# The first group's query and key rows copied inside SBUF, head by head, and four projections moved into the first run of score maxima

## The reference

```
q, k, v = x @ wq.T + bq, x @ wk.T + bk, x @ wv.T + bv     # 16 heads of 8
scores  = einsum('bhqd,bhkd->bhqk', q, k) * 1/sqrt(16)
out     = einsum('bhqk,bhkd->bhqd', softmax(scores), v)
x = layernorm(x + out @ wo.T + bo)
h = silu(x @ w1.T * s1) * (x @ w2.T * s2)                 # 512 wide
h = gelu(h @ h1.T * sh1); h = gelu(h @ h2.T * sh2)
x = layernorm(x + h @ w3.T * s3)
```

## Time and profile before

| What | Value |
|---|---|
| median of 3 runs | 471.40 us (471.39 to 471.72) |
| the profiled execution | 472.66 us, of which the span of the trace is 470.9 us |
| mean granted TensorE clock | 0.992 of full speed |
| PE, DVE, ACT, POOL busy | 450.0, 394.0, 365.5, 86.7 us |
| DMA traffic | 24.48 MB |

### The profile page before, as it was taken

The page is one execution under the profiler, slowest core; times in us unless marked ns, Lnnn a source line. Parts: engine busy times, 40 slices in busy tenths (PEclk is TensorE's granted clock), DMA queues, the critical chain, the costliest instruction groups (busy, mean ns, idle before and its releaser), DMA issues.

```text
span 470.9 us, 9453 instructions
## 1 busy us (share of the span) xinstructions
PE 450.0 (96%) x3630; PEld 213.1 (45%) x3632; DVE 394.0 (84%) x442; ACT 365.5 (78%) x678; POOL 86.7 (18%) x138
## 2 busy tenths in 40 slices
PE   8899999999999999999999999999899799998992
PEld 5333343333333333333343333434343478776882
DVE  6899999999999999999999999999753347647435
ACT  3402898989889899898988989999868786588671
POOL 8400000000000010000000001362511262037002
PEclk9999999999999999999999999999999999999998
...
DMA packets 15547, 24.48 MB, mean 52 GB/s; under 512 B 4560, under 2 KB 8400, under 8 KB 15120
## 3 DMA queue, kind: packets, MB, share of 16 engines
...
...
## 4 chain that ended last, share of the span: by engine, by line
PE 77%; DVE 11%; ACT 5%; issue 2%; POOL 2%; DMA 2%; ACTq 0%; POOLq 0%; DVEq 0%
PE ps L1036 31%; PE ps L1090 29%; PE ps L1174 11%; DVE negmax L798 8%; PE ps L1073 2%; ACT arena L542 2%; DMA qx<-parts_q 1%; ACT hid L582 1%; DVE hf L889 1%; ACT v_pad L576 1%; PE ps L992 1%; PE ps L1123 1%; DVE stats L844 1%; PE ps L1001 1%; ACT hid L592 1%
## 5 line engine op out<-in xcount | busy, mean ns | idle before, releaser
L798 DVE TENSOR_REDUCE negmax<-ps 128x1 f32<-128x1024 f32 x256 | 309.5, 1223 | 6.6 <-PE ps L1036 3.6
L542 ACT ACTIVATE arena<-ps 128x512 f32<-128x512 f32 x512 | 275.1, 597 | 38.9 <-PE ps L1073 15.8
L1036 PE MATMUL ps<-kx,qx 61*128 61x512 f32 x512 | 186.3, 443 | 2.3 <-DMA qx<-parts_q 1.3
L1073 PE MATMUL ps<-qx,kx 64*128 64x512 f32 x512 | 182.2, 450 | 0.0
L1090 PE MATMUL ps<-arena,v_pad 128*32 128x256 f32 x2048 | 163.8, 392 | 1.1 <-ACT arena L542 1.1
L1036 PEld LDWEIGHTS ps<-kx,qx 61*128 61x128 f32 x512 | 75.4, 184 | 101.3 <-DVE negmax L798 85.6
L1090 PEld LDWEIGHTS ps<-arena,v_pad 128*32 128x32 f32 x2048 | 40.5, 108 | 88.1 <-issue 51.3
L1073 PEld LDWEIGHTS ps<-qx,kx 64*128 64x128 f32 x512 | 75.7, 184 | 8.2 <-issue 4.9
L1174 PE MATMUL ps<-hid,w_high 128*128 128x512 f32 (+1 forms) x296 | 67.6, 386 | 1.1 <-ACT hid L592 1.0
L1174 PEld LDWEIGHTS ps<-hid,w_high 128*128 128x128 f32 x296 | 54.3, 188 | 12.6 <-ACT hid L592 1.8
L898 DVE TENSOR_TENSOR hid<-hf,hid 128x512 fp32r<-128x512 f32 x32 | 21.9, 689 | 25.4 <-ACT hid L592 25.4
...
## 6 DMA issues: line engine op xcount, KB each, us to landing
...
```

The lines of the kernel that those rows point to most:

```text
L542: nc.scalar.activation(probs[:, n // HG % 2, heads(n), :], ps[:, PLAN["score", n][0], :], ACT.Exp, scale=SCALE).then_inc(exp_done, 1)
L798: nc.vector.tensor_reduce(negmax[:, t // TURNS % 2, h * QT + q:h * QT + q + 1], ps[:, bank:bank + 2, :], AX.XY, ALU.max, negate=True)\
L1036: ins = nc.tensor.matmul(ps[:, MAX_BANK + 2 * (t % 2) + part, :], qx[at, slot, qc, h, q * P:(q + 1) * P], kx[at, slot, h, part * C:(part + ...
L1073: nc.tensor.matmul(ps[:, bank, :], kx[at, slot, h % PAIR, kt * P:(kt + 1) * P], qx[at, slot, qc, h % PAIR, :], start=True, stop=True)\
```

## The change

Line numbers in this section are those of the changed program where they stand behind a +.

- The first group's rows are no longer stored to DRAM and loaded back. `spread_k` and `spread_q` copy them from SBUF to SBUF, one transfer for each head and part: 8 rows at the source, each read twice, 16 rows at the destination. SP issues 8 for k (64 KB each) and 8 for q of chunk 1 (32 KB each); ACT issues 8 for q of chunk 0 (32 KB each), of which four stand ahead of its fourth high part.
- The first 16 turns take the heads one after the other (`FIRST_HEADS` = 0, 2, 1, 3), and each head has a semaphore (`head_in`), which counts its four transfers.
- Projections 5 to 8 move from ahead of the first turn to behind turns 1, 4, 7 and 10 (`LATE_JOBS`), where they stand in for the fillers; the turn after one has no fillers.
- PE's six fillers wait for the fourth low part. DVE adds the bias of v ahead of that fourth split.
- The two memsets of slot 1 of `qx` go from DVE to POOL, behind `stage_v`.
- The low and high parts lie together in one tensor, `parts`; SP's stores for the other groups are six (k, and q of both chunks) where four stood at this place.

The diff (left out: the move of buffers and semaphore names, and the definition of `store_q_first`, which goes):

```diff
@@ -145,10 +145,14 @@
+FIRST_HEADS = (0, 2, 1, 3)
 WARM, FILL = 9, 6
+LATE_JOBS = (1, 4, 7, 10)
 
 
 def head_of(t):
+    if t < TURNS:
+        return FIRST_HEADS[t // QT], t % QT
@@ -181,18 +187,16 @@
-               for n, at in enumerate((ARENA, ARENA + SLOT_BYTES, ARENA + 2 * SLOT_BYTES, ARENA + 5 * SLOT_BYTES))]
+               for n, at in enumerate((ARENA, ARENA + SLOT_BYTES, ARENA + 2 * SLOT_BYTES, ARENA + 6 * SLOT_BYTES))]
 
         qx = nc.alloc_sbuf_tensor_at("qx", [P, 2, QC, PAIR, C], F32R, offset=ARENA)
         kx = nc.alloc_sbuf_tensor_at("kx", [P, 2, PAIR, L], F32R, offset=ARENA + 2 * QC * PAIR * C * 4)
-        low = arena[0][:, 8 * PAIR * L:].bitcast(F32).rearrange("p (n t) -> p n t", n=2)
 
         attn = arena[1][:, 0:2 * U_ALL * C].bitcast(F32).rearrange("p (u c) -> p u c", c=C)
         probs = arena[1][:, 2 * U_ALL * C:].bitcast(F32).rearrange("p (s h c) -> p s h c", s=2, h=HG)
 
-        prt = sb("prt", [P, 4 * TOK], BF16)
-        high = prt[:, 0:4 * TOK].bitcast(F32).rearrange("p (n t) -> p n t", n=2)
-        part = {n: (high[:, a], low[:, a]) for a, n in enumerate("qk")}
+        parts = nc.alloc_sbuf_tensor_at("parts", [P, HALVES, 2, TOK], F32, offset=ARENA + 2 * SLOT_BYTES)
+        part = {n: (parts[:, 1, a], parts[:, 0, a]) for a, n in enumerate("qk")}
@@ -308,6 +313,12 @@
+        def spread_q(eng, h, j, qc, done):
+
+            at = h // PAIR * GROUP + j * HALVES * DH
+            eng.dma_start(qx[at:at + HALVES * DH, 0, qc, h % PAIR, :].bitcast(F32),
+                          parts[h * DH:(h + 1) * DH, :, 0, qc * C:(qc + 1) * C]).then_inc(done, 16)
+
@@ -370,24 +381,29 @@
-            sp.wait_ge(split_high, 2)
-            store_k(0, 0, 0, 1, k_first)
+            def spread_k(h, j):
+
+                at = h // PAIR * GROUP + j * HALVES * DH
+                sp.dma_start(kx[at:at + HALVES * DH, 0, h % PAIR, :].bitcast(F32),
+                             parts[h * DH:(h + 1) * DH, j, 1, 0:L].unsqueeze(1).broadcast_to([DH, HALVES, L]))\
+                  .then_inc(head_in[h], 16)
+
             sp.wait_ge(split_low, 2)
-            store_k(0, 1, 0, 1, k_first)
-            sp.wait_ge(k_first, STORE_INC)
-            load_k(0, 0)
+            for h in FIRST_HEADS:
+                for j in range(HALVES):
+                    spread_k(h, j)
             sp.wait_ge(split_low, 4)
-            sp.wait_ge(rows_in[0][0], LOAD_INC[0])
-            for i in range(HALVES):
-                store_q(1, i, 0, NG, q_out[1])
-            sp.wait_ge(q_out[1], STORE_INC)
-            load_q(0, 0, 1)
+            for h in range(HG):
+                for j in range(HALVES):
+                    spread_q(sp, h, j, 1, rows_in[0][1])
             for j in range(HALVES):
                 store_k(0, j, 1, NG, k_out[0])
-            for i in range(HALVES):
-                store_q(0, i, 1, NG, q_out[0])
+            for c in range(QC):
+                for i in range(HALVES):
+                    store_q(c, i, 1, NG, q_out[c])
             sp.wait_ge(k_out[0], STORE_INC)
-            sp.wait_ge(q_out[0], STORE_INC)
+            for c in range(QC):
+                sp.wait_ge(q_out[c], STORE_INC)
@@ -517,17 +527,13 @@
-                    act.wait_ge(split_high, n + 1)
-                    store_q_first(0)
-            act.wait_ge(split_low, 3)
-            store_q_first(1)
-            act.wait_ge(q_first, STORE_INC)
-            for r in range(2):
-                for i in range(HALVES):
-                    at = r * GROUP + i * HALVES * DH
-                    act.dma_start(qx[at:at + HALVES * DH, 0, 0].bitcast(F32),
-                                  q_dram[i, 0, 0, r * PAIR:(r + 1) * PAIR].rearrange("h d j t -> (d j) h t"))\
-                       .then_inc(rows_in[0][0], 16)
+                    act.wait_ge(split_low, n + 1)
+                    for h in FIRST_HEADS[:PAIR]:
+                        for j in range(HALVES):
+                            spread_q(act, h, j, 0, head_in[h])
+            for h in FIRST_HEADS[PAIR:]:
+                for j in range(HALVES):
+                    spread_q(act, h, j, 0, head_in[h])
@@ -684,6 +690,12 @@
+            for r in range(2):
+                at = slice(r * GROUP + ROWS, (r + 1) * GROUP)
+                if r == 0:
+                    pool.wait_ge(v_staged, 2)
+                nc.gpsimd.memset(qx[at, 1].bitcast(F32), 0.0).then_inc(rows_set_late, 1)
+                pool.wait_ge(rows_set_late, r + 1)
@@ -773,7 +785,7 @@
-            for n in range(EARLY):
+            for n in range(EARLY - 1):
@@ -785,7 +797,7 @@
-            no_rows(1)
+            split(EARLY - 1)
@@ -1017,10 +1029,8 @@
-            for n in range(EARLY, len(JOBS)):
-                job(n)
-            pe.wait_ge(proj_ready, 1)
-            busy(FILL, FIRST_BANKS[1])
+            pe.wait_ge(split_low, EARLY)
+            busy(FILL, JOB_BANKS[-1])
@@ -1030,9 +1040,14 @@
-                    if t % TURNS == 0:
-
-                        pe.wait_ge(rows_in[slot][qc], (t // (PER * TURNS) + 1) * LOAD_INC[qc])
+                    if t < TURNS and t % QT == 0:
+                        pe.wait_ge(head_in[FIRST_HEADS[t // QT]], 64)
+                    elif t % (PER * TURNS) == 0:
+                        pe.wait_ge(rows_in[slot][qc], t // (PER * TURNS) * LOAD_INC[qc])
+                    elif t % TURNS == 0:
+
+                        first = LOAD_INC[1] if (slot, qc) == (0, 1) else 0
+                        pe.wait_ge(rows_in[slot][qc], (t // (PER * TURNS) + 1) * LOAD_INC[qc] + first)
@@ -1100,14 +1115,20 @@
-                busy(1, FIRST_BANKS[1])
-                busy(1, FIRST_BANKS[1], C // 2)
+                if t in LATE_JOBS:
+                    job(EARLY + LATE_JOBS.index(t))
+                elif t - 1 not in LATE_JOBS:
+                    if t > LATE_JOBS[-1]:
+                        pe.wait_ge(proj_ready, 1)
+                    bank = JOB_BANKS[0 if t > LATE_JOBS[-1] else -1]
+                    busy(1, bank)
+                    busy(1, bank, C // 2)
                 if t == TURNS + 2:
 
                     pe.wait_ge(ident_ready, 3)
                     pe.wait_ge(proj_ready, EARLY)
                     turn_max(0)
-            pe.wait_ge(rows_set, 4)
+            pe.wait_ge(rows_set_late, 2)
```

13 lines of the change are left out of this document (6 added, 7 removed).

## The result

The changed kernel is slower: 474.69 us median (473.46 to 492.66, 5 runs) against 471.39 (471.01 to 471.72, 5 runs), a ratio of 1.006 [1.0044, 1.0076]. This ratio leaves out the executions near 492 us, as a disturbed run would be left out, though here they belong to the kernel (the experiments show it): over all executions of the changed kernel on record they were 7 of 16. Predicted was 468.9, with a range of 468.3 to 472.4.

The account below looks back on a forecast made before the run. A lead-in of the first turn's time plus 23 turns at DVE's pace, then a PE-bound loop. Gain 3.2 less 0.7 for moved projections is 2.5 us, taking the median from 471.4 to 468.9; range 468.3 to 472.4.

Parts of the forecast that it names:

- the first term: Lead-in: four ACT issues at 0.67 us each let the first turn start at 15.4 instead of 18.61, gaining 3.2 us.
- no earlier turn: Rival, lead-in: slow issues or a late fourth transfer keep the first turn from coming earlier; 470.5 to 471.5, chance 0.08.
- The rival of the clock: Lead-in: PE's 1.5 us pause drops the clock, leaving 0.5 to 0.9 us of gain; 469.8 to 471, chance 0.2.
- What follows here is dense: Argument against a clock fall in the lead-in: fillers and full-width products follow PE's 1.5 us pause.
- What the moved projections cost: Behind turns 1, 4, 7 and 10: DVE waits 0.4 us once, then 0.1 each; 0.7 us, bounds 0.2 and 1.3.
- The moved memsets: Lead-in: moving two memsets from DVE to POOL costs nothing; POOL spends 2 x 1.8 us between 12.4 and 16.1.
- SP's queue: Ahead of the loop: stores end between 31.0 and 33.2, ahead of 33.7; costed at nothing, bounds 0 and 5 us.
- the copies didn't hold the stores: Denies the rival that copies ending at 31.2 delay stores and loop start; 471.4 to 476, chance 0.12.
- Head 0's q: Lead-in: head 0's rows complete at 13.8, needed at 15.4, so the first turn doesn't wait for them.
- the first half of the prediction: Lead-in up to the first turn: fillers start at 14.1 and the first turn at 15.4 instead of 18.61.

Follow-up runs that it names:

- e10: Changed kernel with SP's eight transfers of k held back until ACT has issued its first four transfers of q; 494.26 us in one run.
- the trace of 473.38: A later execution of the changed kernel, with no edit, traced; 473.38 us.
- e2: Changed kernel with ACT's fourth high part ahead of all its transfers; 472.11 us, 1.0023 against the kernel before.
- e11: e9 with six fillers behind the second turn; 471.17 us, 0.9995 against the kernel before.
- e9: e5 with the two memsets back on DVE, behind the last split; 490.88 us, 1.0388 against the kernel before.
- e7: Changed kernel with SP alone issuing the k and chunk 0 q transfers, in head order, and ACT chunk 1; 475.04 us in one run.
- e12: e5 with one transfer of head 0's q moved from ACT's queue to SP's, as its third; 475.53 us, 1.0089 against the kernel before.
- e5: Changed kernel with e2's order, late projections ahead of the turns, ACT's copies of them between its transfers; 469.89 us, 0.996 against before.
- the second trace of before: The kernel before the change run once more, with no edit, for another trace; 472.02 us in one run.

## Why the prediction was wrong

**The step that failed** is the first term: "Bounds 0.44 and 0.72, and I take 0.67 with the gap between two. Four of them: 9.76 + 2.7 = 12.5." The rate came from 36 moves that one queue issued by itself. Here SP issued its own transfers at the same time, and the four took 4.97 to 5.46 us with the gaps between them in five traces (5.36 in the trace of the result). e10, one trace, shows 3.48 with SP silent: of the 2.7 us that I missed, 0.8 are ACT's own, mostly a first issue of 1.3, and 1.9 come with SP's transfers. The rows had one issue of 1.44 among 36, and the prediction gave "no earlier turn", which asked for 1.2 us per issue on both queues, 0.08. On ACT's queue it was so, 1.32 on average; on SP's it wasn't, 0.93. A slip on top: worked through, the bounds 0.44 and 0.72 give a first turn at 15.3 and 15.6, because the split can't start before 13.3, and not "15.0 to 15.9".

In the trace of 473.38 the first turn came 3.5 us later than predicted. The fillers began at 16.23 instead of 14.1, which is 2.1 of it, and at half clock the turn came 2.66 us behind their start instead of 1.24, which is the other 1.4.

**The rival of the clock** was the right second step with the wrong size. I had reckoned with a pause of 1.5 us and with a fall worth 1.6 to 2 us. The pause was 3.7 to 4.6 us in five traces, because the high part stood behind the issues, and in four of them the fall began in it. When the clock came back within 3.4 us, mostly the fillers paid for it. When it didn't, the first real score came 19 us late. The range ended at 472.4, so neither kind of execution was in it. "What follows here is dense" was held against a fall; dense it was, 52.7 busy of 54.5 us, and the clock stayed at half for all of them.

**What the moved projections cost** was mis-sized: 0.7 us predicted, bounds 0.2 and 1.3, measured 1.67, 1.68 and 1.68 in three kernels. (The upper bound was also added up wrongly: four times 0.4 is 1.6.) DVE's timeline of e2 from 16 to 45 us has it, as the idle time ahead of its reductions:

```profile
17.10 2.36 DVE L806 TENSOR_REDUCE negmax<-ps 128x1 f32<-128x1024 f32 x2 [3.19 <-PE ps L1047]
19.93 3.49 DVE L806 TENSOR_REDUCE negmax<-ps 128x1 f32<-128x1024 f32 x3 [0.47 <-PE ps L1047]
23.69 3.49 DVE L806 TENSOR_REDUCE negmax<-ps 128x1 f32<-128x1024 f32 x3 [0.28 <-PE ps L1047]
27.46 3.49 DVE L806 TENSOR_REDUCE negmax<-ps 128x1 f32<-128x1024 f32 x3 [0.28 <-PE ps L1047]
31.22 14.80 DVE L806 TENSOR_REDUCE negmax<-ps 128x1 f32<-128x1024 f32 x13 [0.27 <-PE ps L1047]
```

Against DVE's pace of before, the first projection delays it by 0.56 us, where I had 0.4, and the later three by 0.37 each, where I had 0.1. I took the projection at 0.86 from a stretch where projections followed each other; behind a turn it takes 1.05 (20.80 to 21.85 in the trace of 473.38). One group of three turns takes 3.76 us there (23.92 to 27.68) instead of 3 x 1.135 = 3.41.

**The moved memsets cost nothing** where they are now; that was right. The step added that without this cover POOL would be late. It didn't ask for the other side, what DVE would do without the move: with the first turn at 16.8 they would cost 1.4 us by DVE's time (e11) and 20 us by the clock (e9).

**SP's queue was costed right**, at nothing: the loads of the second group started at 32.42 and 32.21 in the two traces, predicted 31.0 to 33.2, and no turn of the real loop waited for them. So the copies didn't hold the stores until 31.2. In the trace of 473.38 the last of them landed at 24.3, where I had taken 23.5, and the DMA traffic from 13 to 17 us, when nothing but the copies was under way, was

```profile
DMA packets 200, 0.43 MB, mean 108 GB/s; under 512 B 66, under 2 KB 66, under 8 KB 200
```

That is above the 65 to 98 GB/s which I had taken. (From 9 to 13, when the first ones had just been issued, it was 36.) The prediction had also worked out, from the Trainium skill's page "SBUF — State Buffer", section on the DMA port swizzle, that the copies would take until 29.2. The single move's 49 GB/s agrees with that page's 54 for two ports; the 108 GB/s of transfers of several heads in flight don't keep to it. But e7 and e12 show how near the limit is: with the loads at 35.8 and 36.0 instead of 32.5, PE waited 1.5 and 3.3 us, and lost more to the clock.

**Head 0's q** was taken to be complete at 13.8; its second transfer was issued at 11.16 in e5 and landed 4.98 us later, at 16.14. The heads didn't go one after the other at 49 GB/s: by 16.14 the queues had moved 0.48 MB in the trace of 473.38, more than two heads' rows, but mixed. In the changed kernel the late landing was hidden behind the late high part; in e2 and e5 it is what the first turn waits for.

**The base.** The trace of before had its first turn at 18.61; another has 17.98.

In sum, for the trace of 473.38: the first turn at 18.89 and not 15.4, between it and the first real score 27.72 and not 26.6, 46.61 instead of 42.0. The edit that comes nearest to the first half of the prediction is e2's, and e5 with both mended is at 468.3 to 468.9 where the clock stays up. That this is the predicted 468.9 is luck: it comes by another kernel and another way, the first turn at 16.3 and nothing lost behind it.

**Open.** Which pause brings the clock down, and for how long. e2 idled 1.67 and 0.93 us and none of 10 executions fell; e9 idled 0.32 and 1.22 us and four of four did. The changed kernel came back in 3.4 us once, after 54.6, 58.0 and 51.2 us other times, and once after 27.3 us, for 3.4 us only. Ahead of the fall the traces differ little: the products of v start at 8.78 in the short execution and at 8.48 to 8.57 in the four long ones. With one short trace that is no rule. Nor is it settled why e2, whose first real score (43.91) is level with the second trace of before (43.84), comes out at 1.0023; nine of its ten executions have the mean clock (0.991 or 0.992) that goes with the stretch near 340, and of the 21 executions of before beside it only 13 have 0.991 to 0.993. Among those the medians are 472.1 and 471.75, so this accounts for about half of the 0.74 us between the medians and leaves the rest open.
